# Two short attentions of a decoder kernel: output projection moved to the front of its tick, residual addition moved ahead of the same tick's maximum

## The reference, cut to what matters

```python
# 8 sequences, 100 tokens, 16 heads of 8
Q = (x @ Wq.T).reshape(B, S, HKV, G, HEAD_DIM)          # HKV = 4, G = 4
K = (x @ Wk.T).reshape(B, S, HKV, HEAD_DIM)
V = (x @ Wv.T).reshape(B, S, HKV, HEAD_DIM)
scores = jnp.einsum('bskgd,bswkd->bskgw', Q, K_win) * scale
attn = jax.nn.softmax(scores, axis=-1)
out = jnp.einsum('bskgw,bswkd->bskgd', attn, V_win)
return out @ Wo.T

# the causal one, with L = 100 queries, the first S keys of the context
sm = jnp.einsum('nlhd,nshd->nlhs', q, k) / math.sqrt(D)
sm = jnp.where(causal_mask[None, :, None, :], -jnp.inf, sm)
attn = jnp.einsum('nlhs,nshd->nlhd', jax.nn.softmax(sm, axis=-1), v)
return attn.reshape(N, L, H * D) @ Wo.T + bo

x = x + _L0_attn_ref(_layernorm(x), ...)                # sublayer 1
x = x + _L1_xattn_ref(_layernorm(x), ctx_1024, ...)     # sublayer 5
```

## Time and profile before

| | |
|---|---|
| runs shown, median (lowest to highest) | 1163.63 us (1161.76 to 1164.21) |
| the profiled execution | 1168.05 us, of which the span from first to last instruction is 1166.3 us |
| mean granted TensorE clock in it | 0.85 of full speed |
| busy: TensorE matmul, VectorE, ScalarE, GpSimd | 914.9, 756.6, 570.1, 255.2 us |
| ticks of L0a | from 18.9 to 91 us |
| ticks of L1x | from 510.7 to 590.8 us |

### The profile page before, as it was taken

The page is one execution under the profiler, slowest core; times in us unless marked ns, Lnnn a source line. Parts: engine busy times, 40 slices in busy tenths (PEclk is TensorE's granted clock), DMA queues, the critical chain, the costliest instruction groups (busy, mean ns, idle before and its releaser), DMA issues. The chain is left out here.

```text
span 1166.3 us, 18306 instructions
## 1 busy us (share of the span) xinstructions
PE 914.9 (78%) x6163; PEld 567.9 (49%) x6163; DVE 756.6 (65%) x2181; ACT 570.1 (49%) x1660; POOL 255.2 (22%) x349
## 2 busy tenths in 40 slices
PE   5985599999878465168866879885786999999986
PEld 2344499999746222133544358554582233333323
DVE  6457667777658289364577745632647888888823
ACT  3236367777541311032353533452252677777773
POOL 4006245555400022021302000134400111111100
PEclk8698699999979678565986779798695899999997
DMA  9500000000000620100001000553022011111000
GB/s 236 144 1 1 0 2 2 1 2 2 1 1 1 84 29 0 28 1 1 2 1 32 19 1 1 149 133 90 15 45 64 1 25 26 26 26 20 2 1 15
DMA packets 76177, 35.83 MB, mean 31 GB/s; under 512 B 35226, under 2 KB 74562, under 8 KB 76083
## 3 DMA queue, kind: packets, MB, share of 16 engines
q1 hardware_dynamic: 73714, 33.61, 13.2%
q0 software_dynamic: 896, 0.63, 0.2%
q10 hardware_dynamic: 1472, 0.41, 0.2%
HBM read 24.42 MB, written 11.05 MB: 30 GB/s over the span
## 5 line engine op out<-in xcount | busy, mean ns | idle before, releaser
L527 ACT ACTIVATE L3x_E<-L3x_pS 128x400 f32<-128x400 f32 (+1 forms) x384 | 167.8, 507 | 48.9 <-PE L3x_pS L621 48.0
L443 DVE TENSOR_REDUCE L3x_NMP<-L3x_pM 128x1 f32<-128x361 f32 x384 | 178.1, 525 | 19.0 <-PE L3x_pM L599 18.0
L599 PE MATMUL L3x_pM<-ctx_tm 64*128 64x361 bf16 x384 | 104.4, 341 | 14.0 <-DVE L3x_NMP L443 9.9
L621 PE MATMUL L3x_pS<-ctx_tm 64*128 64x400 bf16 (+1 forms) x384 | 107.6, 350 | 3.4 <-ACT L3x_E L527 2.1
L1473 ACT ACTIVATE L0x_E<-L0x_E,ctx_r 128x100 f32<-128x100 f32 x288 | 105.1, 369 | 9.6 <-DVE L0x_E L1380 9.6
L636 PE MATMUL L3x_pO<-L3x_E,CT 128*32 128x400 f32 (+1 forms) x768 | 85.5, 517 | 0.0
L599 PEld LDWEIGHTS L3x_pM<-ctx_tm 64*128 64x128 bf16 x384 | 30.4, 96 | 110.4 <-DVE L3x_NMP L443 91.1
L1562 PE MATMUL L0x_pU<-ctx_tm,L0x_E 128*100 128x129 f32 x576 | 70.5, 279 | 2.9 <-POOL L0x_E L1293 2.9
L1552 PE MATMUL L0x_pS<-L0x_QS,CT 128*128 128x100 f32 x576 | 70.8, 281 | 0.0
L1562 PEld LDWEIGHTS L0x_pU<-ctx_tm,L0x_E 128*100 128x100 f32 x576 | 67.2, 171 | 4.5 <-POOL L0x_E L1293 4.0
L1293 POOL TENSOR_TENSOR L0x_E<-L0x_E,L0x_RZ 128x1200 f32<-128x1200 f32 x24 | 52.7, 2194 | 75.0 <-DVE L0x_RZ L1400 75.0
(11 more groups left out here) (631 smaller groups left out, 2126.7 us busy)
## 6 DMA issues: line engine op xcount, KB each, us to landing
ctx_tm<-in_ctx SPq DMA_DIRECT2D x8, 704.0 KB
ctx_tm<-key_terms SPq DMA_DIRECT2D x16, 270.8 KB, 4.4
key_terms<-ctx_tm SPq DMA_DIRECT2D x42, 90.2 KB
ctx_tm<-in_L_ffn_wi SPq DMA_DIRECT2D x4, 512.0 KB, 8.1
ctx_tm<-in_L_ffn_wo SPq DMA_DIRECT2D x4, 512.0 KB
ctx_tm<-query_terms SPq DMA_DIRECT2D x16, 75.0 KB, 3.7
slots_in<-L2a_zeros SPq DMA_DIRECT2D x8, 129.0 KB
L2f_XS<-slots_in SPq DMA_DIRECT2D x4, 258.0 KB, 3.1
```

The source lines that it names most:

```text
L443: nc.vector.tensor_reduce(NMP[:, p, i // NC4, a, i % NC4:i % NC4 + 1], v, AX.X, ALU.max, negate=True).then_inc(s_mr, 1)
L527: nc.scalar.activation(E[0:r, n % EB, :], pS[0:r, n % 3, 0:NG * T], ACT.Exp, scale=SCALE8).then_inc(s_e, 1)
L599: nc.tensor.matmul(pM[:, n % 3, 0:CW], key_rows(QS, a)[:, b, p, 128 * x:128 * x + 128], key_rows(KS, a)[:, b % KB, c, p, :], start=True, s ...
L621: nc.tensor.matmul(pS[0:NW[k], n % 3, 0:NG * T], key_rows(KS, a)[:, b % KB, k % 4, p, 128 * (k // 4):128 * (k // 4) + NW[k]], key_rows(QS, ...
```

## The change

On TensorE `project(b)` is called at the front of tick 2b+11, ahead of `max_scores(t)`, in place of behind `turn_maxima` and ahead of `token_major`. On VectorE `residual(b)` is called at the front of the same tick, ahead of `maximum(t)`, in place of behind it. No wait, buffer or instruction is added or removed, and ScalarE, GpSimd and the DMA queues keep their lists. Both calls of `attention_short` get it.

```diff
@@ VectorE
                 for t in range(LAST + 1):
+                    for b in range(B):
+                        if t == 2 * b + PROJ_AT:
+                            residual(b)
                     if t < N:
                         maximum(t)
@@
                         if t == 2 * b + TM_AT:
                             normalised(b)
-                        if t == 2 * b + PROJ_AT:
-                            residual(b)
                         if t == 2 * b + PROJ_AT + 1 and b < B - 1:
                             stats(b)
@@ TensorE
                 for t in range(LAST + 1):
+                    for b in range(B):
+                        if t == 2 * b + PROJ_AT:
+                            project(b)
                     if t < N:
                         max_scores(t)
@@
                     for b in range(B):
-                        if t == 2 * b + PROJ_AT:
-                            project(b)
                         if t == 2 * b + TURN_AT:
                             turn(b)
```

## The result

The kernel after took 1153.76 us in the median of 5 runs (1153.34 to 1163.50), against 1163.20 us for 5 runs of the kernel before beside it (1161.34 to 1164.21): ratio 0.9938, interval 0.9909 to 0.9968. The five runs are four within 0.7 us of each other and one, the profiled one, 9.5 us above them. Its span is 1161.8 us, against 1166.3 before, at a mean granted clock of 0.841 in place of 0.850. Both profiles are thus of long executions: this one is the longest of its five, and the profiled one of the kernel before (1168.05 us) is longer than all five of its runs.

A forecast was written before the change was run, and what follows sets the result against it. No engine is full; a ring of hand-overs bounds the kernel. Gains of 2.49 us in L0a and 2.42 in L1x make 4.9 us off the median: 1158.7 us, range 1156.4 to 1162.0, forecast's chance 0.73.

The forecast's parts named there:

- ring by ring: In L0a and L1x, the cycle of hand-overs between engines that sets a pair of ticks; gains of 2.49 and 2.42 us.
- The sum for L0a: All gains and losses over L0a's projection ticks, from tick 11 on, added up to 2.49 us.
- the first front: First projection tick (11): the projection ahead delays max_scores by 0.07 us in L0a, 0.42 in L1x.
- the two pairs: Two pairs of ticks with maxima: gain 0.58 us each in L0a, 1.16 together; 1.38 for two in L1x.
- tick 15: In L0a, score(11) comes at f+2.81 in place of f+3.44, a gain of 0.63 us.
- the ticks from 16 on: Fronts of ticks 17 and 19 lose 0.35 us each, the ticks gain 0.53 and 0.94: 0.77 in each stage.
- A pair with maxima: Time from one f to the next: 5.30 us for 5.88 in L0a, 5.67 for 6.36 in L1x.
- f: Start of max_scores on TensorE in an odd tick that has a projection; other times are counted from it.
- The residual addition is hidden: On VectorE ahead of the maximum, its 0.28 us costs nothing; without cover at most 0.7 us over six ticks.
- Rival 1: In both stages exps doesn't hold score(t-4), so more comes back: 6.7 us in all, 1156.9 us; chance 0.06.
- Rival 3: Projections at ten fronts cost 3.8 us and nothing comes back, as token_major doesn't set the pair: 1167.4 us; chance 0.06.
- Rival 2: Later stages give half back as TensorE's clock rises later against the work: gain 2.4 us, 1161.2 us; chance 0.15.

The follow-up runs named there:

- turn_first: Kernel after with turn_maxima also ahead of max_scores; mean 1153.53 us on the third chip (0.9939 to before), 1154.70 us on the fourth (0.9921).
- after_again: Kernel after, unchanged, run again on the first chip of the experiments; mean 1156.49 us, ratio 0.9946 to the kernel before.
- the halves: Both moves made in only one of the stages L0a and L1x, against the kernel before; L0a alone 1160.87 us (0.9984), L1x alone 1160.92 us (0.9983).
- after_late_busy: Kernel after with four VectorE copies behind each of the two stages and seven more TensorE products beside them; mean 1176.23 us, 1.0087 to before.
- l1x_only: Projection and residual addition moved in L1x alone, L0a as in the kernel before; mean 1160.92 us, ratio 0.9983.
- l1x_end_4: Kernel before with four more VectorE copies (2.4 us) at the end of L1x; mean 1167.05 us, ratio 1.0027.
- l1x_end_8: Kernel before with eight more VectorE copies (4.8 us) at the end of L1x; mean 1170.72 us, ratio 1.0064.

## Why the prediction was right or wrong

**Right, ring by ring.** The sum for L0a was 2.49 us, the window at full clock shows 2.39. The sum is closer than its terms, whose errors partly cancel: the first front cost 0.15 us for 0.07, the two pairs gave 1.22 for 1.16, tick 15 gave 0.74 for 0.63, and the ticks from 16 on 0.58 for 0.77. A pair with maxima was to take 5.30 us in L0a and took 5.28; 5.67 in L1x, and took 5.76. The projection holds TensorE 0.39 us, not the 0.32 that I chose (0.45 in L1x; in `turn_first`, where turn_maxima follows it, 0.30: 51.68 to 51.98): the choice between 0.28 and 0.46 fell too near the stream of eight passes, and the 81 ns a matmul that the Trainium skill gives for a sustained stream of 128 columns (TensorE: Matmul & The Clock Gate, Back-to-back issue gap) is little over half of what a pass of 144 columns took in that stream (0.14 us). That the pair came out at 5.28 all the same is in part luck. exps started at f+1.82 (59.41) and not at f+1.91, so score came at about f+2.71 and not f+2.81, and these 0.10 us made up for the longer projection. The residual addition is hidden, as said, with 0.47 us to spare. L1x was to give 2.42 and gave 1.85 to 1.92. Of the 0.57 missing in `after_again`, 0.22 are its two pairs (1.16 for 1.38), and 0.47 the ticks from 16 on (from score to the last residual addition 20.55 us for 20.85, a gain of 0.30 where I had 0.77), in part because its last projection ran at the lower clock (0.75 us for 0.46); the first front cost 0.35 and not 0.42. The rings give 4.2 to 4.3 us for 4.9.

**Right, the rivals that fell.** Rival 1 (exps doesn't hold score) is out in this kernel, for the row names exps, although exps did start earlier than f+1.91, which the rival had as its condition. With `turn_first`, where exps started at f+1.17, the pair was 4.95 us. Rival 3 is out: its price a front is real (0.05 + 0.39 = 0.44 us for 0.37), but token_major did move.

**Wrong: the step from the stages to the whole.** The failed sentence is "Nothing in the blocks behind either stage waits for more than the stage's end, so both gains should arrive there whole". Nothing was found that waits for more, yet a gain doesn't arrive as it is. By the means the change is worth 7.2, 6.5, 4.4 and 7.8 us on four occasions, 6.5 on average, for 4.3 us in the rings. Of the four intervals only the last (5.6 to 9.5 us) leaves 4.3 out; for their average I estimate 5.0 to 7.6 from them. Delays show it more plainly: 2.4 us cost 6.1 behind L0a, 4.8 us cost 7.4, 4.7 us cost 11.1, all three beyond their intervals; 2.4 us behind L1x cost 3.7, within it. In the eighteen traces of this study L1f took 43.0 to 43.2 us eight times and 45.6 to 46.1 ten times, L2x 67.1 to 67.7 fourteen times and 69.9 four times, none between, with their code the same in all. Rival 2 named a mechanism that the traces do show, a rise of the clock that comes at another place of the work. It summed it to half of the gain given back, where the traces show 2.5 us a stage, to either side. It had no place for what isn't the clock, such as the 4.7 us over which L1a varies. The range followed from that: its lower end had half a us for all that I didn't know. Its rule that "each us that a rise comes later costs 0.5 us" fits: the products of L2x that met no rise ran 5.13 us at half speed and lost 2.45.

**Wrong: the spread.** From three runs 2.45 us apart I took the metric to be good to 0.2%. The kernel before alone went from 1158.2 to 1169.4 us over the four chips of the experiments, with means of 1160.6, 1163.0, 1163.3 and 1165.0. In each of the four, its runs with a mean granted clock of 0.853 and above took 2.9 to 3.7 us less than those of 0.849 and below (1162.21 against 1165.48 on the first chip, 15 and 7 runs): a difference between runs of one kernel that goes with the clock. The kernel after doesn't follow this everywhere. On the second chip it does (above), but on the fourth its two shortest runs (1153.33 and 1153.73) had 0.850 and 0.849 and the longest three 0.851 to 0.853, and the four runs near 1153.7 us in the first comparison had 0.847 to 0.849. So the mean clock alone doesn't tell a short run from a long one. In that first comparison four of the five runs after agreed with each other, and the fifth was 9.5 us off; by the means of the same runs it is 7.2 us.

**Open.** Why the mean effect is larger than the work that was moved: by 1.5 for the change and for the two delays behind L1x, by 2.4 and 2.5 for the other two delays, but by nothing for the halves (2.1 us each, whose intervals would allow 1.5 too). That stages take two durations explains that a gain may come out 2.5 us a stage larger or smaller, not that it comes out larger on average. `after_late_busy` was meant to touch this and failed. One lead is L1a: it took 116.9 us on average in the four traces of the kernel after and 118.1 in the four in which everything ahead of L1a is as before (the kernel before, `l1x_only`, `l1x_end_4` and `l1x_end_8`). These 1.2 us would be half of what is missing for the change. The long product on VectorE is in one of the first four and in three of the second. But they are few traces, and with four copies behind L0a of the kernel before L1a was short as well (116.8), in the kernel that came out 6.1 us slower.

## What to carry to other kernels

In a pipeline of in-order engines, write out the ring of hand-overs with its times and the next two rings behind it: that gave the new pair to 0.02 us in L0a, by some luck, and to about 0.1 in L1x. Two moves that each break one side of a ring are worth next to nothing singly (6.02 and 5.78 us for 5.88) and 0.60 us together, so a step shouldn't be dropped because it gains nothing alone. From the stage to the whole, add a term for the clock: look in the trace for stages that begin at 1.2 GHz with much for TensorE to do, give each the price of its first products at either clock (here 2.45 us), to both sides, look for stages that wait for a transfer too, and measure over chips, not over three runs on one.

## What the runs showed of the hardware that I had not expected

A stage's duration can be one of two values, with the same instructions: L2x 67.4 or 69.9 us, L1f 43.1 or 45.7, in eighteen traces. In L2x what differs is whether the granted clock rises from 0.50 to 1.00 ahead of a long group of products or behind it; in L1f the clock was 0.78 to 0.79 in the short ones and 0.65 to 0.69 in the long. In one pair of traces the L2x that started 1.2 us later was the shorter one, by 2.47 us. Other stages spread without such a difference of clock: L1a 114.9 to 119.6 us, with one product on VectorE that took 2.9 to 3.0 us for 0.3 in ten traces of eighteen, and the stage behind L2x 73.0 to 78.9, its two ends being two executions of `turn_first` at clocks of 0.83 and 0.82. Two passes of a float32 product of 128 columns held TensorE 0.39 us up to the start of max_scores, 0.45 ahead of L1x's mask product and 0.30 ahead of turn_maxima in `turn_first`; a pass in a stream of eight took 0.14. And one kernel's mean differs by 4.4 us between chips, as much as the two rings gave.
